# Attention and mixture-of-experts kernel: row maxima in one ScalarE transfer, early inputs, layer 2's mask on VectorE

## The reference

```python
# layer 2 (layer 3 is the same without the mask, and with an output projection)
q = split_heads(query @ Wq.T + bq)      # query = layernorm(x)
k = split_heads(key @ Wk.T + bk)        # key = value = ctx_1024, [8, 256, 256]
v = split_heads(value @ Wv.T + bv)
scores = jnp.einsum('bhqd,bhkd->bhqk', q, k) / np.sqrt(DK).astype(jnp.float32)
scores = jnp.where(mask[:, None, :, :] == 0, jnp.float32(-1000000000.0), scores)
p_attn = jax.nn.softmax(scores, axis=-1)
x = jnp.einsum('bhqk,bhkd->bhqd', p_attn, v)
# layer 1: scores masked to 0, convolved 3x3 per head with a softmaxed kernel,
# masked to -inf, softmax, times v, output projection
x = x + block(_layernorm(x, axis=-1), ...)
```

## Time and profile before

| | |
|---|---|
| median of 3 runs | 2540.61 us (2532.79, 2540.61, 2540.71) |
| the profiled execution | 2542.26 us, its span 2540.5 us |
| TensorE busy | 2044.3 us, 80% |
| VectorE busy | 1307.0 us, 51% |
| ScalarE busy | 842.3 us, 33% |
| GpSimd busy | 737.2 us, 29% |
| granted TensorE clock, mean | 0.88 |
| DMA engines, packets of SP's and ACT's queue | 27.3% of 16 engines' span |

### The profile page before, as it was taken

How to read it: one execution, slowest core, us unless ns; L and a number is a source line. 1 busy time by engine, 2 the same in 40 slices (tenths; PEclk the granted TensorE clock), 3 DMA queues, 4 the chain that set the end, 5 groups by cost and what they waited for, 6 DMA issues and landing times. The chain is left out here.

```text
span 2540.5 us, 41393 instructions
## 1 busy us (share of the span) xinstructions
PE 2044.3 (80%) x13605; PEld 1660.4 (65%) x13605; DVE 1307.0 (51%) x3958; ACT 842.3 (33%) x2000; POOL 737.2 (29%) x928
## 2 busy tenths in 40 slices
PE   6869979992799999998589748995895953887694
PEld 5657746661698989987589735664684832554594
DVE  3532225524688888886400156765346445675423
ACT  4613313422133333333333223453341421345321
POOL 1022100005344444454111122310546743231132
PEclk9969989985899999999699969995796986898797
DMA  2052130002211111100199534426576653442384
GB/s 79 9 207 63 53 114 13 1 1 77 84 35 42 43 44 43 38 20 7 60 354 335 206 111 123 134 71 233 158 146 235 176 107 101 117 118 57 141 310 155
DMA packets 142732, 280.78 MB, mean 111 GB/s; under 512 B 20160, under 2 KB 99008, under 8 KB 138432
## 3 DMA queue, kind: packets, MB, share of 16 engines
q1 hardware_dynamic: 125824, 232.49, 27.3%
q0 software_dynamic: 16704, 45.64, 7.7%
HBM read 218.94 MB, written 56.62 MB: 108 GB/s over the span
## 5 line engine op out<-in xcount | busy, mean ns | idle before, releaser
L1956 PE MATMUL heads_ps_c<-heads_band,heads_sT 128*128 128x129 f32 x3072 | 368.9, 277 | 14.4 <-DVE heads_band L2175 13.4
L1956 PEld LDWEIGHTS heads_ps_c<-heads_band,heads_sT 128*128 128x128 f32 x3072 | 355.0, 192 | 24.7 <-issue 22.9
L2112 POOL TENSOR_SCALAR heads_band<-heads_shifts,heads_taps 128x130 f32<-128x130 f32 x384 | 251.1, 668 | 254.5 <-PE heads_ps_c L1956 250.3
L506 POOL DMA_INDIRECT weights_xg<-xn_rows,token_of x197 | 189.9, 964 | 449.3 <-DVE token_of L686 192.8
L2175 DVE SCALAR_TENSOR_TENSOR heads_band<-heads_shifts,heads_taps,heads_band 128x130 f32<-128x130 f32 x768 | 226.7, 351 | 18.4 <-POOL heads_band L2112 13.7
L2049 ACT ACTIVATE heads_probs<-heads_mixes,heads_least 128x256 f32<-128x256 f32 x256 | 116.1, 500 | 343.8 <-DVE heads_least L2188 343.8
L1697 DVE TENSOR_REDUCE heads_negmax<-heads_ps_m 128x2 f32<-128x512 f32 x256 | 169.6, 688 | 83.6 <-PE heads_ps_m L1553 81.3
L1654 ACT ACTIVATE heads_probsT<-heads_ps_e 128x512 f32<-128x512 f32 x256 | 147.1, 596 | 196.2 <-PE heads_ps_e L1577 195.8
L1032 PE MATMUL experts_ps_g<-weights_w,experts_xT 128*128 x504 | 135.0, 392 | 3.1 <-ACT experts_xT L1082 2.5
L1055 PE MATMUL experts_ps_y<-weights_w,experts_hT 128*128 (+1 forms) x486 | 133.6, 383 | 1.1 <-DVE experts_y L1117 1.1
L1167 POOL DMA_INDIRECT combine_yg<-y_rows,slot_of x48 | 45.4, 946 | 300.7 <-SPq L66 286.7
(11 more groups left out here) (386 smaller groups left out, 4245.4 us busy)
## 6 DMA issues: line engine op xcount, KB each, us to landing
experts_w<-in_experts_dram SPq DMA_DIRECT2D x23, 2180.0 KB, 10.0
weights_w<-in_experts_dram SPq DMA_DIRECT2D x16, 1536.0 KB
weights_w<-in_experts_dram SPq DMA_DIRECT2D x32, 768.0 KB, 6.4
piece_rows<-heads_pieces SPq DMA_DIRECT2D x96, 192.0 KB, 2.7
y_rows<-experts_y SPq DMA_DIRECT2D x125, 128.0 KB, 1.9
heads_stackQ<-piece_rows SPq DMA_DIRECT2D x48, 192.0 KB
heads_stackK<-piece_rows SPq DMA_DIRECT2D x48, 192.0 KB
weights_w<-in_experts_dram SPq DMA_DIRECT2D x8, 1088.0 KB
```

The costliest lines, as they stand in the source:

```text
L506: pool.indirect_dma_start(self.xg[:, u, :], None, xn_dram, bass.IndirectOffsetOnAxis(ap=tb.token_of[:, j:j + 1], axis=0)).then_inc(self.x_ ...
L1956: last = pe.matmul(out[:, qc * SEQ + k0:qc * SEQ + k1], sT[:, h % 2, kc, qc * P + dq:qc * P + dq + P], band[:, h % 2, dq, w0:w0 + k1 - k0] ...
L2112: last = pool.tensor_scalar(band[:, h % 2, dq, :], shifts[:, 0, :], taps[:, r % 2, h, dq * TAPS:dq * TAPS + 1], None, ALU.mult)
```

## The change

1. `w`, `bv`, the context and the mask buffer move into a class `HeadInputs`, whose tiles live in a stage around both the combine stage and the heads stage: `layer1`, which exists, and two new ones, `layer2` and `layer3`. The combine stage's SyncE issues the first loads (`load_first`: w, bv, contexts 0 and 1, mask 0) at its start.
2. In heads2 and heads3 SyncE's order before the rounds is: put 0, stack 0, put 1, context 2, stack 1, put 2, stack 2, (mask 1), put 3.
3. `place_max` is one DMA of the three rows, issued by ScalarE after the exponential of head 3. The wait count is 16 a use instead of 48.
4. stackK's constant rows are written by two ScalarE copies at the start of the stage instead of by VectorE's memset; they are −1 in heads2. TensorE's scoreT waits for them (`rows_set`).
5. Before the rounds, the value projections of TensorE and their placing by VectorE come one round later.
6. In heads2 the mask matmul L1550 goes; VectorE adds the mask with two `tensor_tensor_reduce` for each head, and keeps the maximum, not negated.
7. In heads1 the context has two buffers. Both are filled at the stage's start, and `context(1)` between stack 0 and put 1 goes.

```diff
+class HeadInputs:
+    def load_first(self, sp):
+        sp.dma_start(self.w[:, :], self.w_dram).then_inc(self.w_loaded, 16)
+        if self.ctxT is not None:
+            sp.dma_start(self.bv[:, :], self.w_dram[0:1, 3 * DC * D + 2 * DC:].to_broadcast([P, D]))\
+                .then_inc(self.bv_loaded, 16)
+            for b in range(2):
+                self.load_context(sp, b)
+        if self.mask is not None:
+            self.load_mask(sp, 0)
...
-            if masking:
-                load_mask(0)
-            for u in range(3):
-                put_pieces(u)
-                stack(u)
+            put_pieces(0)
+            stack(0)
+            put_pieces(1)
+            context(2)
+            stack(1)
+            put_pieces(2)
+            stack(2)
             if masking:
                 sp.wait_ge(maskT_ready, 1)
-                load_mask(1)
+                inputs.load_mask(sp, 1)
             put_pieces(3)
-            context(2)
-            place_max(0)
             for u in range(ROUNDS):
                 if u % 2 and (u + 5) // 2 < B:
                     context((u + 5) // 2)
                 if u + 3 < ROUNDS:
                     stack(u + 3)
-                if u + 1 < ROUNDS:
-                    place_max(u + 1)
...
-                if masking:
-                    pe.matmul(out, ident16[:, :], mask_add[:, 0, b % 2, :], start=True, stop=False,
-                              skip_group_check=True)
...
-                if u < 3:
-                    project_value(u, 0)
-            pe.wait_ge(constants, 2)
+                if u > 0:
+                    project_value(u - 1, 0)
+            pe.wait_ge(constants, 1)
...
+            def constant_rows(r0, r1):
+                act.activation(stackK[STACK:STACK + PIECES, r0:r1, :, :].rearrange("a r j n -> a (r j n)"),
+                               ones[STACK:STACK + PIECES, 0:1].to_broadcast([PIECES, (r1 - r0) * HALF * SEQ]),
+                               ACT.Copy, scale=-1.0 if masking else 1.0).then_inc(rows_set, 1)
...
+            def place_max(u):
+                r = u % SLOTS
+                act.wait_ge(rows_ready, u + 1)
+                act.dma_start(stackQ[STACK:STACK + PIECES, r, :, :].rearrange("a j (q n) -> a (j q) n", q=QC),
+                              max_rows[:, :]).then_inc(max_placed[r], 16)
...
+                    if h == 3 and u + 1 < ROUNDS:
+                        place_max(u + 1)
...
-            v.memset(stackK[STACK:STACK + PIECES, :, :, :], 1.0).then_inc(constants, 1)
...
+            def masked_max(u, h):
+                n, b = HALF * u + h, u // 2
+                v.wait_ge(scored, n + 1)
+                if h == 0:
+                    v.wait_ge(mask_ready, b + 1)
+                if n >= 2:
+                    v.wait_ge(maxed, n - 1)
+                for qc in range(QC):
+                    m = QC * h + qc
+                    last = v.tensor_tensor_reduce(out=masked[:, h % 2, qc, :],
+                                                  in0=ps_m[:, h % 2, qc * SEQ:(qc + 1) * SEQ],
+                                                  in1=mask_add[:, 0, b % 2, qc * SEQ:(qc + 1) * SEQ], scale=1.0,
+                                                  scalar=-3.0e38, op0=ALU.add, op1=ALU.max,
+                                                  accum_out=negmax[:, m:m + 1])
+                last.then_inc(maxed, 1)
...
-            sp.dma_start(ctx[:, :, :], xnT[:, :, 0:SEQ]).then_inc(ctx_loaded, 16)
+            for b in range(2):
+                sp.dma_start(ctx[:, b, :, :], xnT[:, :, b * SEQ:(b + 1) * SEQ]).then_inc(ctx_loaded[b], 16)
...
             put_pieces(0, 0)
             stack(0, 0)
-            context(1)
             put_pieces(0, 1)
```

More of the change, by code:

```diff
@@ L1146, in _, with combine_norm_stage @@
                 sp.wait_ge(stored[p], 16 * ((NT + YB - 1 - p) // YB))
-def combine_norm_stage(core, name, K, tb, y_dram, x, xn, xnT, ident, eps):
+def combine_norm_stage(core, name, K, tb, y_dram, x, xn, xnT, ident, eps, prefetch):
     GT, DEEP = 4, 8
@@ L1159, in combine_norm_stage, with _ @@
         block = s.block()
+        @block.sync
+        def _(sp):
+            prefetch(sp)
         @block.gpsimd
@@ L1359, with __init__, load_mask, load_context @@
 VW = LANE
-def split_heads_stage(core, name, mode, xnT, ctxT, w_dram, dst, ident, ident16, ones, piece_rows,
-                      mask=None):
+class HeadInputs:
+    def __init__(self, s, w_dram, ctxT=None, mask=None, mask_type=I32):
+        self.w_dram, self.ctxT, self.mask = w_dram, ctxT, mask
+        WB = 3 * DC * D
+        self.w, self.bv = s.sb("w", [P, WB + 2 * DC + D]), s.sb("bv", [P, D])
+        self.ctx = s.sb("ctx", [P, 2, DC, SEQ])
+        self.mask_in = None if mask is None else s.sb("mask_in", [P, 2, QC * SEQ], mask_type)
+        self.w_loaded, self.bv_loaded, self.mask_loaded = (s.sem(n) for n in ("w_loaded", "bv_loaded", "mask_loaded"))
+        self.ctx_loaded = [s.sem(f"ctx_loaded{p}") for p in range(2)]
+    def load_mask(self, sp, b):
+        sp.dma_start(self.mask_in[:, :, :].rearrange("p a n -> p (a n)"), self.mask[b * P:(b + 1) * P, :])\
+            .then_inc(self.mask_loaded, 16)
+    def load_context(self, sp, b):
+        sp.dma_start(self.ctx[:, b % 2, :, :].rearrange("p c n -> p (c n)"), self.ctxT[b * P:(b + 1) * P, :])\
+            .then_inc(self.ctx_loaded[b % 2], 16)
+    def load_first(self, sp):
[7 more added lines that the diff above has]
+            self.load_mask(sp, 0)
+def split_heads_stage(core, name, mode, xnT, inputs, dst, ident, ident16, ones, piece_rows):
     WB = 3 * DC * D
@@ L1394, in split_heads_stage @@
         ps_v, ps_r = ps_vr[:, 0:QC * P], ps_vr[:, QC * P:QC * P + P // 2].bitcast(BF16)
[L1395 to L1398, removed]
+        split_steps, qk_free, rows_set = (s.sem(n) for n in ("split_steps", "qk_free", "rows_set"))
+        constants, written = s.sem("constants"), s.sem("written")
         projected, v_projected, qk_taken, v_placed = (s.sem(n) for n in
@@ L1767, in _, with conv_heads_stage @@
             finish(ROUNDS - 1)
-def conv_heads_stage(core, name, xnT, w_dram, dst, ident, ident16, ones, mask, kernels, piece_rows):
+def conv_heads_stage(core, name, xnT, inputs, dst, ident, ident16, ones, kernels, piece_rows):
     WB = 3 * DC * D
@@ L1883, in sequence @@
                 if more:
-                    context(2 * i + r // 2 + 1)
+                    context(i, r)
                 put_pieces(i, r + 1)
@@ L1926, in project_value @@
                     for c in range(DC):
-                        last = pe.matmul(out, ctx[:, c, tc * P:(tc + 1) * P], wv[:, c, p * P:(p + 1) * P],
+                        last = pe.matmul(out, ctx[:, (r // 2) % 2, c, tc * P:(tc + 1) * P], wv[:, c, p * P:(p + 1) * P],
                                          start=(c == 0), stop=(c == DC - 1))
@@ L2722, in build @@
                           biased=True, ahead=4, first=first)
-        combine_norm_stage(core, "combine1", 1, tb, y_dram[0:NT * P, :], x, xn, xnT, ident, eps[:, 0:1])
-        split_heads_stage(core, "heads2", MASKED, xnT, i["ctxT"], i["heads2"], x, ident, ident16, ones,
-                          piece_rows, mask=i["mask2"])
+        with Stage(core, "layer2") as layer2:
+            inputs = HeadInputs(layer2, i["heads2"], i["ctxT"], i["mask2"])
+            combine_norm_stage(core, "combine1", 1, tb, y_dram[0:NT * P, :], x, xn, xnT, ident, eps[:, 0:1],
+                               inputs.load_first)
+            split_heads_stage(core, "heads2", MASKED, xnT, inputs, x, ident, ident16, ones, piece_rows)
         NT = TILES * 2 + 31
```

90 lines of the change are left out of this document (39 added, 51 removed).

## The result

The changed kernel took 2522.52 us in the median (2519.77 to 2524.96), the kernel before 2540.66 us beside it: 0.9934 of it, 95% interval 0.9909 to 0.9959. That is 18.1 us off, where 20.5 were forecast. In two later batches it stood at 0.9943 (0.9924 to 0.9962) and 0.9915 (0.9898 to 0.9933). Its profiled execution took 2524.96 us with a span of 2523.1 us.

What follows compares the result with a forecast made beforehand. A DMA chain of stack rows and pieces was taken to bound heads3's rounds, with TensorE much closer to it in heads2. −5.6 − 5.0 − 3.1 − 3.0 − 5.0 + 1.2 = −20.5 us gave 2520.1; range 2504 to 2537.

Steps and rivals of the forecast that it cites:

- SyncE's queue is not the bound of heads3; a chain of stack rows and pieces is: heads3's rounds of 11.20 us wait for bytes to land; relieving SyncE of 1.6 us a round is worth 0.
- If the maxima are early it waits for the stack instead.: heads3: TensorE's 1.64 us a round of waiting on the maxima would turn into waiting for the stack.
- the sign that I named, waits now after piece_rows: heads3: TensorE's waits named after piece_rows, with stack issues still 11.2 to 11.5 us apart, would show the forecast right.
- The merged transfer costs 0.2 us a round: Maxima in one transfer instead of three: 0.2 us a round, +2.2 over heads3's 11 rounds, the same in heads2.
- rival D: The merged maxima queue on few DMA engines with the stack, scoreT comes 2.3 us later a round: 2566, 6%.
- the chain of transfers binds: heads2 after the change: transfers set the round at 11.9 us, above VectorE's 10.1 and TensorE's 10.4.
- the pair's price: heads2, VectorE: two add-and-reduce take 0.70 us against 0.65 for one reduce; bounds 0.05 to 0.7 more.
- Rival C: heads2's rounds stay at 12.2 us, from VectorE paying 0.7 or the mask staying in the way; 2526, 16%.
- heads2's rounds and tail: heads2: eleven rounds of 12.18 − 11.9 give −3.1 us, the part after the last stack −3.0.
- Openings: Inputs loaded by the stage in front: first matmuls earlier by 5.0 us in heads1, 5.4 in heads2, 5.5 in heads3.
- Prefetch beside the gathers: Combine stages: prefetched bytes running beside the gathers cost +0.5 us, bounds 0 to +3.
- the context taken out of the opening: heads1: the second context no longer between stack 0 and the second put, −0.6 us.

Runs made afterwards that it cites:

- max1_sp: The changed kernel with the maxima still in one transfer, but issued by SyncE in its old place instead of ScalarE; 0.9912 of the kernel before.
- max3_sp_b: The changed kernel with the maxima in three transfers issued by SyncE, second measurement; 0.9905 of the kernel before (first batch 0.9906).
- max3_act: The changed kernel with the maxima in three transfers instead of one, still issued by ScalarE; 0.9893 of the kernel before.
- no_prefetch: The changed kernel with the first input loads issued at the start of the heads stages, not in the combine stages; 0.9986 of the kernel before.

## Why the prediction was right, point by point

**SyncE's queue is not the bound of heads3; a chain of stack rows and pieces is.** Right, and shown twice: moving the maxima back to SyncE costs nothing (max1_sp, max3_sp_b), spreading the loads takes 41 us off. For heads3 the two neighbouring intervals of the earlier trace rows were enough to see it.

**"If the maxima are early it waits for the stack instead."** In the changed kernel they are not early: TensorE still waits 1.64 us a round before scoreT, and so the sign that I named, waits now after piece_rows, did not come. Where they are earlier, in max3_act, the sentence holds: 0.7 us a round less before scoreT, 0.66 for the stack, and the stacks as far apart as before. With the loads spread both waits are gone.

**The merged transfer costs 0.2 us a round.** heads3's steady rounds went from 11.20 to 11.36, 11.34 and 11.05 us in three executions. The size fits two and not the third; it stays open. TensorE's wait before scoreT does say that the one transfer lands later than three by the same issuer, 1.64 against 0.95 us a round, which is rival D's mechanism; but the chain covers it, and its price is far below the 1.1 us from which D decides.

**heads2: "the same chain is at work", "the chain of transfers binds", 11.9.** The size was right by luck (11.76), the reason wrong on both sides of the change. Before, TensorE was busy for all 134.0 us of the eleven rounds, so its own work was the 12.18, and the chain lay under it. After, I had TensorE's own work at 12.18 − 1.75 = 10.4; it was busy for 118.69/11 = 10.8 us a round, and with its wait for VectorE, whose mask preparation is stuck behind GpSimd, that makes 11.7; the chain lies under that at about 11.4. The failed step is VectorE's load: I added the pair's price, which was right (0.35 us from one half to the next, as in heads1), to a mean over the round, and didn't look at where in the round VectorE's instructions meet GpSimd's. Rival C named VectorE, for the wrong price.

**heads2's rounds and tail.** −6.1 forecast; the stretch behind the first projection moved by −6.3, but made up otherwise. The rounds gave 11 × 0.42 = −4.6 where −3.1 was forecast. The part behind the last stack gave −0.6 where −3.0 was forecast (−2.0 and −2.9 in the two other executions), and the way to the first steady stack gave −1.1 where +0.4 was. The errors cancel.

**Openings.** −15.9 forecast for the three first projections; −14.9 by the marks. I charged the two more stage ends 0.34 each; the gap behind heads3 went from 2.09 to 2.50 us.

**Prefetch beside the gathers.** +0.5 forecast, 0 to +3 as bounds; it came to about 3 us (against no_prefetch and against before alike), nearly all in combine1, whose first rows came 4.3 us later. This is the term that was most undersized: with it, the sum is −18 instead of −20.5, which is what was measured. The terms of heads2 are off too and cancel, so the close agreement is in part luck.

**heads1.** −0.6 forecast for the context taken out of the opening; +1.0 seen in a stretch that scatters from 557.3 to 561.1 us over the fourteen executions at hand. These can't be told apart.

## What to carry to other kernels

When a queue's transfers come at even intervals, look whether the next one waits for bytes to land or for the queue: two neighbouring rounds in which a transfer was issued at different times decide it. If it is the bytes and the DMA share is far from 1, split repeated loads, as here into copies of 16 rows, before touching who issues what. Ask the same question in every stage anew: heads2 has the same transfers as heads3, but there TensorE was busy all the time, and the chain did not bind. A load moved into the stage in front competes with that stage's own first loads: here the short combine stage gave back about 3 of the 18 us.

## What the runs showed of the hardware

Splitting a load that repeats 16 rows three times or twice into single copies of 16 rows took the round from 11.36 to 9.33 us, with the stage's mean DMA share going from 0.35 to 0.49 and the time with just two or three packets in flight from 3.9 to 0.5 us a round. Three more issues by SyncE each round did not show.

A VectorE instruction of 0.43 us took 0.74 or 1.30 us by when in GpSimd's instruction of 1.16 us it started; both end 0.28 us after GpSimd's, and TensorE waits 0.97 us in each round with the long one.
